# Experts, full batches and cross-attention in one block per engine, and fewer unread products in three pauses

## What is computed

```python
x = x + _L0_xattn_ref(ctx_1024, _layernorm(x))   # distances, dynamic time warping, rows of ctx added along the path
x = x + _L0_ffn_ref(_layernorm(x), gate, W1, b1, W2, b2)   # 16 experts, 3 of them for each row
x = x + _L1_xattn_ref(ctx_1024, _layernorm(x), mask, ...)  # cross-attention over 722 masked rows and the 100 own ones
x = x + _L1_ffn_ref(_layernorm(x), ...)                    # 4 low-rank variants of one layer, the best 2 for each row
```

```python
raw_gate = jax.nn.softmax(jnp.einsum('btd,de->bte', x, gate), axis=-1)
_, topk_idx = jax.lax.top_k(raw_gate, 3)
hidden = jax.nn.relu(jnp.einsum('btd,edh->bteh', x, W1) + b1)
expert_out = jnp.einsum('bteh,ehd->bted', hidden, W2) + b2
return jnp.einsum('bte,bted->btd', gate_topk, expert_out)
```

## Time and profile before

| | |
|---|---|
| median of 3 runs | 1208.29 us (1207.68 to 1208.56) |
| the profiled execution | 1209.34 us, span from first to last instruction 1207.7 us |
| mean granted TensorE clock | 0.950 |
| TensorE (PE) busy | 1074.1 us, 89% of the span |
| VectorE, ScalarE, GpSimd busy | 460.0, 336.7 and 224.6 us |
| DMA traffic | 152.84 MB, mean 127 GB/s |

### The profile page before, as it was taken

One profiled execution on the slowest core, in us unless ns is written; L12 is line 12 of the kernel. 1 busy time (PEld: TensorE's weight loads), 2 busy tenths in 40 slices (PEclk: granted clock), 3 DMA queues, 4 the chain that ended last, 5 costly groups with the idle time before them and its releaser, 6 DMA issues. The chain is left out here.

```text
span 1207.7 us, 17529 instructions
## 1 busy us (share of the span) xinstructions
PE 1074.1 (89%) x5498; PEld 702.9 (58%) x5499; DVE 460.0 (38%) x1698; ACT 336.7 (28%) x802; POOL 224.6 (19%) x341
## 2 busy tenths in 40 slices
PE   8966679937949999999999999949999999999997
PEld 8952235524448777677766777635446665555554
DVE  7847888883570000000000010036765463121212
ACT  4424756770001222222222222214245430000000
POOL 0963021110021121121111111210030001121211
PEclk9978799968969999999999999969999999999999
DMA  8876005128404575856596555560021005000000
GB/s 302 227 169 219 1 1 183 53 99 220 152 14 164 156 246 183 283 193 218 182 311 201 182 182 183 173 196 10 0 77 64 1 1 157 1 1 1 14 14 28
DMA packets 71763, 152.84 MB, mean 127 GB/s; under 512 B 12026, under 2 KB 16258, under 8 KB 70870
## 3 DMA queue, kind: packets, MB, share of 16 engines
q1 hardware_dynamic: 63454, 131.21, 32.0%
q0 software_dynamic: 6928, 17.04, 6.3%
q10 hardware_dynamic: 1320, 3.84, 1.2%
HBM read 131.83 MB, written 20.25 MB: 126 GB/s over the span
## 5 line engine op out<-in xcount | busy, mean ns | idle before, releaser
L1305 ACT ACTIVATE att<-phid,b 128x128 f32<-128x128 f32 x216 | 79.3, 367 | 306.8 <-PE phid L1274 306.8
L1327 DVE TENSOR_TENSOR att<-py,att 128x512 f32<-128x512 f32 x27 | 18.7, 692 | 367.3 <-PE py L1282 367.3
L1274 PEld LDWEIGHTS phid<-tiles,shared 128*128 128x128 f32 x896 | 111.5, 192 | 37.4 <-issue 37.4
L1274 PEld LDWEIGHTS phid<-tiles,Wmem 128*128 128x128 f32 x832 | 103.5, 192 | 39.1 <-issue 39.1
L1274 PE MATMUL phid<-tiles,shared 128*128 x896 | 114.4, 276 | 1.2 <-issue 0.5
L1274 PE MATMUL phid<-tiles,Wmem 128*128 x832 | 106.3, 276 | 5.8 <-issue 4.5
L1282 PE MATMUL py<-shared,att 128*128 128x512 f32 x224 | 110.0, 593 | 0.0
L1282 PE MATMUL py<-Wmem,att 128*128 128x512 f32 x208 | 102.3, 594 | 0.4 <-DMA att<-in_b 0.4
L2365 PE MATMUL acc<-tiles 128*128 128x400 f32 x256 | 90.6, 505 | 0.0
L2431 DVE SCALAR_TENSOR_TENSOR tiles<-bf,shared 128x400 f32<-128x400 f32 x64 | 32.4, 567 | 130.3 <-PE bf L2350 129.6
L2324 PE MATMUL bf<-shared,Wmem 128*128 128x400 f32 x192 | 70.0, 501 | 2.0 <-PEq L49 1.3
(11 more groups left out here) (388 smaller groups left out, 1715.5 us busy)
## 6 DMA issues: line engine op xcount, KB each, us to landing
Wmem<-in_W SPq DMA_DIRECT2D x16, 2048.0 KB, 14.2
shared<-in_W SPq DMA_DIRECT2D x16, 2048.0 KB, 11.9
cT<-in_ctxT SPq DMA_DIRECT2D x8, 1444.0 KB, 11.8
ctx_rows<-in_ctx SPq DMA_DIRECT2D x8, 1280.0 KB
Wmem<-in_Wkv SPq DMA_DIRECT2D x2, 2048.0 KB, 9.2
att<-in_b SPq DMA_DIRECT2D x16, 256.0 KB, 14.3
tiles<-in_WoT SPq DMA_DIRECT2D x4, 1024.0 KB
Wmem<-in_WiT SPq DMA_DIRECT2D x3, 1024.0 KB, 7.1
```

Of the source, the lines that this page charges most:

```text
L1274: ins = pe.matmul(ph[j % NH][:, :], W1[u][:, k, j * P:(j + 1) * P], xgT[:, bass.ds(w, 1), k * P:(k + 1) * P].rearrange("p o t -> p (o t)") ...
L1305: act.activation(hT[:, j, :], ph[j % NH][:, :], ACT.Relu, bias=b1[:, bass.ds((e + u) * HJ + j, 1)]).then_inc(relu_ok, 1)
```

## The change

Four things.

1. `experts` and `attend_full` no longer open blocks. They become `expert_parts` and `full_batches`, which return one function for each engine; `attend` calls them at the head of its own streams. So the two block ends (L1185 and L1880) with their clearings are gone. The banks of PSUM are shared with `attend`'s; the tiles of the full batches lie in the room of the queries.
2. The flag is still read by each engine, now behind its last expert work. If it is not set, the body is branched over. VectorE increments a new semaphore `full_over` behind that, and the four other engines wait for it. TensorE then reads the number of tiles from the table and waits for the last `y_free`. VectorE's two memsets and GpSimd's constant are only made if the flag is set; `qk_scale` is computed on VectorE behind the experts.
3. The unread products ahead of `attend`'s first transpose become 20 (18 before), behind that wait.
4. Three other pauses have fewer: 13 for 18 at the start of `distances`, 12 for 18 ahead of the first path product, 18 for 36 ahead of the table product.

```diff
@@ distances, TensorE
-            keep_awake(pe, pbb[0], ident, 18)
+            keep_awake(pe, pbb[0], ident, 13)
@@ route, TensorE
             pe.wait_ge(p_out[0], 16)
-            keep_awake(pe, px_whole[1], ident, 18)
+            keep_awake(pe, px_whole[1], ident, 12)
...
             pe.wait_ge(over_ok, 1)
-            keep_awake(pe, px_whole[0], ident, 36)
+            keep_awake(pe, px_whole[0], ident, 18)
             pe.wait_ge(of_ok, 2)
@@ experts
-def experts(nc, io, res):
-    ctx = ExitStack()
-    with ctx:
-        sb, pb, sem = allocator(nc, ctx)
+def expert_parts(io, res, sb, sem, bank):
...
-        banks = [pb(f"phid{i}", [P, D]) for i in range(NH)]
-        ph = [bank[:, 0:P] for bank in banks]
-        py = pb("py", [P, D])
-        ptx = [pb(f"ptx{i}", [P, KD * P]) for i in range(2)]
+    ph = [bank[i][:, 0:P] for i in range(NH)]
+    py = bank[4]
+    ptx = bank[5:7]
...
-        block = ctx.enter_context(nc.Block())
...
+    return y_free, expert_sp, expert_pe, expert_act, expert_pool, expert_dve
@@ attend
+        y_free, expert_sp, expert_pe, expert_act, expert_pool, expert_dve = expert_parts(io, res, sb, sem, bank)
+        full_sp, full_pe, full_act, full_pool, full_dve = full_batches(io, res, sb, sem, bank, qT[:, :, :].rearrange("p k n -> p (k n)"))
         block = ctx.enter_context(nc.Block())
...
         def _(sp):
+            expert_sp(sp)
+            full_sp(sp)
...
         def _(pool):
+            expert_pool(pool)
+            full_pool(pool)
...
-            keep_awake(pe, sum_b, ident, 18)
+            expert_pe(pe)
+            full_pe(pe)
+            last = pe.value_load(res["table"][0:1, E_N:E_N + 1], min_val=E_N, max_val=SLOT_TILES)
+            pe.wait_ge(y_free, last + 1)
+            keep_awake(pe, sum_b, ident, 20)
             turn(0)
...
+            expert_act(act)
+            full_act(act)
             root(0)
...
+            expert_dve(dve)
+            dve.wait_ge(res["vec_in"], 48)
+            link(dve.scalar_tensor_tensor(qk_scale[:, :], gammas[:, 0:1], -DH ** -0.5, gammas[:, 1:2], ALU.mult, ALU.mult))
+            full_dve(dve)
             for m in range(B // 2 + 1):
@@ attend_full
-def attend_full(nc, io, res):
+def full_batches(io, res, sb, sem, bank, spare_cols):
...
-        q = sb("q_d", [S, D])
-        qT = sb("qT_d", [P, KD, S])
-        prT = sb("prT_d", [P, NT, S])
-        o, oT = sb("o_d", [S, D]), sb("oT_d", [P, KD, S])
+    q, o = part(D)[0:S, :], part(D)[0:S, :]
+    qT, oT = (part(KD * S).rearrange("p (k s) -> p k s", k=KD) for i in range(2))
+    prT = part(NT * S).rearrange("p (t s) -> p t s", t=NT)
...
-        def each_full(eng, body):
+    def each_full(eng, body, first=None):
             some = eng.value_load(res["flag"][0:1, B:B + 1], min_val=0, max_val=1)
             with eng.If(some == 1):
+            if first is not None:
+                first()
...
             each_full(sp, body)
+        sp.wait_ge(full_over, 1)
...
             each_full(pe, body)
+        pe.wait_ge(full_over, 1)
...
             each_full(act, body)
+        act.wait_ge(full_over, 1)
...
-            each_full(pool, body)
+        each_full(pool, body, first)
+        pool.wait_ge(full_over, 1)
...
-            each_full(dve, body)
+        each_full(dve, body, first)
+        dve.sem_inc(full_over, 1)
@@ build
-        experts(nc, io, res)
-        attend_full(nc, io, res)
         attend(nc, io, res)
```

More of the change, by code:

```diff
@@ new lines, in full_batches, with part @@
+    ident, x_sb = res["ident"], res["x"]
+    Wq, Wkv, Wo = res["Wq"], res["Wkv"], res["Wo"]
+    vec, qk_scale = res["vec"], res["qk_scale"]
+    stats, mv, rstd = sb("stats_d", [P, NT, 6]), sb("mv_d", [P, NT, 2]), sb("rstd_d", [P, NT])
+    spare = [res["tiles"][:, B + i * NT:B + (i + 1) * NT, :] for i in range(3)]
+    rows = spare[0]
+    vals = spare[1]
+    lnT = spare[2].rearrange("p t d -> p (t d)")[:, 0:KD * NKD].rearrange("p (k n) -> p k n", k=KD)
+    cuts = [0]
+    def part(n):
+        cuts.append(cuts[-1] + n)
+        return spare_cols[:, cuts[-2]:cuts[-1]]
@@ new lines, in full_batches @@
+    took = sem("took_d")
+    bt, b0, b1, p0, p1, bo = bank[0:6]
+    d_in, batch_done, pe_turn, dve_turn, ask_act, act_did, ask_pool, pool_did, hset = (sem(n) for n in (
+        "d_in", "batch_done", "pe_turn", "dve_turn", "ask_act", "act_did", "ask_pool", "pool_did", "hset"))
+    full_over = sem("full_over")
+    cols = [P * t for t in range(CT)] + [C]
+    def each_full(eng, body, first=None):
+        some = eng.value_load(res["flag"][0:1, B:B + 1], min_val=0, max_val=1)
+        with eng.If(some == 1):
+            if first is not None:
+                first()
+            with eng.Fori(0, B) as b:
+                f = eng.value_load(res["flag"][0:1, bass.ds(b, 1)], min_val=0, max_val=1)
+                r = eng.value_load(res["runs"][0:1, bass.ds(b, 1)], min_val=0, max_val=B - 1)
+                with eng.If(f == 1):
+                    body(b, r)
@@ new lines, in full_act, with body, full_pool, first @@
+    def full_act(act):
+        def body(b, r):
+            act.wait_ge(ask_act, (HEADS + 1) * r + 1)
+            act.activation(rstd[:, :], rstd[:, :], ACT.Sqrt).then_inc(act_did, 1)
+            for h in range(HEADS):
+                act.wait_ge(ask_act, (HEADS + 1) * r + h + 2)
+                act.activation(pr[:, :], sc[:, :], ACT.Exp, bias=least[:, 0:1], scale=-1.0, accum_out=total[:, h:h + 1]).then_inc(act_did, 1)
+        each_full(act, body)
+        act.wait_ge(full_over, 1)
+    def full_pool(pool):
+        def first():
@@ L2120, in body @@
+            for t in range(NT):
+                take()
+                dve.tensor_copy(rows[0:KR[t], t, :], b0[0:KR[t], :])
+                dve.drain()
+                unit(rows[0:KR[t], t, :], KR[t])
                 give()
                 take()
-                dve.tensor_copy(oT[:, :, :], bt[:, :].rearrange("p (k s) -> p k s", k=KD)[:, :, 0:S])
+                dve.tensor_copy(vals[0:KR[t], t, :], b0[0:KR[t], :])
+                give()
+            take()
+            dve.tensor_copy(q[:, :], b0[0:S, :])
```

645 lines of the change are left out of this document (297 added, 348 removed).

## The result

| | before | after |
|---|---|---|
| median | 1207.99 us (1207.40 to 1208.56, 4 runs) | 1195.30 us (1192.97 to 1196.96, 4 runs) |
| profiled execution, its span | 1209.34, 1207.7 | 1194.54, 1192.9 |
| mean granted TensorE clock | 0.950 | 0.954 |

The ratio of after to before is 0.9894, 95% interval 0.9875 to 0.9912: 12.7 us less by the medians, 10.6 to 15.1 by the interval. The forecast was 14.8 less (1193.5).

What follows compares the result with a forecast made beforehand. TensorE was taken to bound the kernel, with one 18.75 us hole between experts and attention. Terms 9.5 + 4.0 + 1.3 + 0 = 14.8 us gave 1193.5 us against the median shown, 1208.29; range 1190.5 to 1198.5.

Steps and rivals of the forecast that it cites:

- The merge, up to the first turn: Between experts and attention: one block instead of three starts the first turn 9.8 us earlier, 9.5 us kept.
- The landing of x: Start of attention: the first load of x is back 4.5 us after issue, at 793.5, bounded by 792.4 and 798.5.
- The cover: Behind the experts: flag reads and branches (TensorE 4.79 us, VectorE 3.2) lie under GpSimd's scatter, with 0.6 us to spare.
- Rival A: Attention's start: first wait longer through late x, stalls in the open or falling clock; merge gives 4.5 to 7.5; chance 0.20.
- rival E: Attention's start: GpSimd's DRAIN or full_over waits act as a barrier before x; merge gives 2 us or less; chance 0.03.
- The clock term: First value rows: new TensorE pauses may halve the clock for 3 us, 1.5 us lost; 0.3 taken off.
- The table pause: Ahead of the table product: 18 for 36 unread products starts it 4.0 us earlier, GpSimd's third product being late next.
- The path pause: Ahead of the first path product: 12 for 18 unread products ends them 1.27 us earlier, 1.3 us kept.
- The first pause: Start of distances: 13 for 18 unread products gives 0, as ctx's load decides, down to a loss of 0.5 us.
- B: Larger gain: x lands at 792.4 and the clock rises earlier in the routing stage; 1190 to 1191.5 us; chance 0.12.
- C: Three shortened pauses lose the clock; the stage behind pays half of 3 to 7 us; 1195.5 to 1197; chance 0.07.
- D: Expert loops: moved code makes a backward branch fetch, 3.1 us each; slower than before, 1218 us; chance 0.03.

Runs made afterwards that it cites:

- two_blocks: Kernel before without its block of full batches, qk_scale computed behind VectorE's expert work, experts keeping their own block: 1203.06 us, ratio 0.9939 to the kernel before.
- no_flag: Changed kernel without the flag's reads, branches and bodies, a semaphore from VectorE in their place: 1200.88 us, ratio 0.9927 to the kernel before.
- pauses_only: Kernel before with only the three shorter pauses (13, 12 and 18 unread products), no merge: 1205.58 us, ratio 0.9961 to the kernel before.
- filled_b: Changed kernel with 26 unread products for 20 ahead of attention's first turn and 5 behind the first two turns, repeated in the third group: 1198.14 us, ratio 0.9900.
- filled: Changed kernel with 26 unread products for 20 ahead of attention's first turn and 5 more before the first value rows: 1197.87 us, ratio 0.9907 to the kernel before.
- filled_more: Changed kernel with 26 and 5 unread products around attention's first turns, plus 5 ahead of the expert loops and 5 at attention's end: 1197.03 us, ratio 0.9892.
- undo_first: Changed kernel with 18 for 13 unread products at the start of distances: 1197.13 us, ratio 0.9907 to the kernel before.
- control_b: Changed kernel unaltered, measured again in the group of the kernels that put back one old count: 1196.91 us, ratio 0.9907 to the kernel before.
- control: Changed kernel unaltered, measured again beside its two halves: 1200.62 us, ratio 0.9919 to the kernel before.
- merge_only: Changed kernel with the three old counts put back (18, 18, 36) and the merged block kept: 1202.88 us, ratio 0.9935 to the kernel before.
- three undo kernels: Changed kernel with one old count put back each: 18 at the start of distances, 36 ahead of table, 18 ahead of path: 1197.13, 1199.73, 1197.52 us.

## Why the prediction was right, and where it wasn't

**The merge, up to the first turn.** Predicted 9.8, measured 10.28. The load of x as start, TensorE's products 0.1 behind it (0.03), the turn 8.7 behind it (8.16): all there. The landing of x was taken as 4.5 us; it was 3.96 in after and 3.9 to 5.0 over the other merged kernels. The estimate from the earlier trace rows was close though of another transfer, which is some luck. What the step had wrong is its input: it counts from `x_back[0]` alone, and the second pair's load held VectorE in six of eleven profiles. In after it didn't. The page "DMA: Bandwidth & Descriptors" of the Trainium skill (HWDGE ordering), by which each DMA engine consumes the descriptors of x before those of the keys behind them, is not contradicted: with 16 such loads issued from 784 on, the first pair never landed later than 5.0. Whether they delay the second pair (up to 7.31) no run shows.

**The cover.** TensorE's branch was taken as 4.79 and was 3.88; VectorE's `full_over` came 3.8 us behind its last expert work (4.15 taken), of which its branch was 3.0 (3.2). The margin was 1.1 us, 0.6 forecast. two_blocks and no_flag bound it from both sides: the flag's block as a whole, with its memsets, its branches and its end, costs 7.0, and flag and branches behind the experts nothing. Rival A's part of stalls in the open and rival E are out. The page "Runtime: NRT & Kernel Launch" of the Trainium skill (Instruction fetch mechanics), by which a taken branch to code that isn't loaded waits for a fetch, was cited for that stall; the branch stalls on TensorE whether its target is the end of a block (4.79) or the code behind (3.88).

**The clock term: mis-sized.** The step said that 3 us of value rows might run at half speed, 1.5 us lost, but took off only 0.3. Measured: 1.7 to 2.1 when it happens, and it happened in 6 of 8 profiles. The mechanism, its place and its price were named; its likelihood was read from one row (the pause of 1.95 in the earlier trace rows) and set too low. It should have gone into the sum in full: 9.8 - 1.5 = 8.3 for the merge. By the traces the merge is worth 7.0 (behind the load of x), by the medians 6.5 to 7.9: that is about rival A's size (4.5 to 7.5), in after by the last of its three causes and not by the landing or the branches, and beside it by the late fall below.

**What the sum didn't hold.** Short falls of the clock in stages that the change doesn't touch. At the first expert products: from there to the load of x it is 407.2 to 407.9 with the clock kept, 408.4 to 409.2 without it, some 1.2 us, in 8 of the 14 profiles, pauses_only among them (not in before, nor in after). At the pause of 1.00 ahead of the output projection, or that of 1.5 ahead of the feed-forward's first products: 1.2 to 1.9 more than before from the queries to the end (3.2 for two falls), in all eight profiles of merged kernels without fillers, in two_blocks and in filled_b (twice), and not in before, pauses_only, filled and filled_more. The same pause of 1.0 stands in the kernel before without a fall. The count speaks for the merge bringing it about, by the moment at which the pause now comes; filled_b, against filled of the same code, shows that it isn't the code alone. It stays open. With the fall at the value rows (1.7) it is what the first comparison lacks: 12.7 by the medians and 12.80 between the profiles from the path pause on, where 14.8 was forecast. That the profiled spans as a whole differ by 14.8 is luck, a sum of errors: 2.0 more than the change explains ahead of the path pause (the first store of the path lay between 272.4 and 280.7 over the runs, with the same code ahead of it but for one count), 0.7 more at the path, 0.5 more at the turn, against 1.7 and 1.5 of clock.

**The table pause.** Predicted 4.0 with GpSimd late next; 4.17 between the profiles, 3.25 when undone, GpSimd the releaser in every one. What was not seen: the gain depends on when the clock rises under the long version.

**The path pause.** Predicted 1.3; 2.0 between the profiles, 0.64 when undone, for the same reason.

**The first pause.** Predicted 0, "down to a loss of 0.5"; the medians of undo_first and control_b are 0.2 apart, which is nothing. Its risk shows only when ctx comes late: at 16.56 in pauses_only and 17.73 in filled_b the pauses of 1.98 and 2.77 were followed by products 1.6 us longer. With ctx at 15.8 to 16.0 and pauses of 1.2 to 1.6 the clock held, with 13 products (control, control_b) as with 18 (merge_only). No profile with 18 products had ctx as late as 16.56, so what they would have saved isn't shown.

**Rivals.** B (larger): x didn't land before 3.9. C: the mechanism exists (previous paragraph), but none of the three undo kernels was faster than control_b, so it has no price in the medians. The products right behind the path and table pauses ran at full clock. The fall at the first expert products, 1 of 4 with the old table pause and 7 of 9 with the new one, stays a possible price of some 1.2 us. D: the expert stage is as long as before where the clock is alike, 407.47 before and 407.40 after; no fetch in a loop.

**A small miss.** ScalarE's table load was put before the first input. It came behind a wait, as the timeline of ScalarE in the kernel after shows, and the square root behind it was ready at 788.60, just as VectorE went on (788.63): it cost nothing, with no margin.

```profile
787.10 1.28 ACT L1672 ACT_TABLE_LOAD   x1 [15.02 <-DVE rstd_l L1762]
```

## What to carry to other kernels

A block end costs what its slowest engine has still to finish: here 4.48 us of GpSimd's DRAIN behind an indirect DMA and 4.8 us of TensorE's branch over code that isn't used, and in the merged kernel neither is on the path: the DRAIN is gone from this place and the branch lies under a transfer. When a stage is released earlier, look at what TensorE now waits for in small pieces: pauses of 1 to 1.5 us that were hidden behind a late start come into the open, and the clock may take back what it took here, 1.7 of 10.3 us at the first place and 1.2 to 1.9 at a later one. Count that at its full price, not at a fraction. Before a late start is put down to a missing or an added filler, read the releaser of the late row: here it was VectorE behind the loads of x in every merged profile. And products issued to hold the clock should end when the next late input arrives: what goes beyond is path, as the table and path pauses show (3.25 and 0.64 us when undone). The shorter rows cost nothing that the medians here can show; the profiles leave 1.2 us open.

## What was not expected of the hardware

- Pauses of 1.2 to 1.4 us on TensorE were followed by about 3 us at the low clock in most executions and not in others of the same program, with pauses nearly as long (5.34 against 3.65 us for the same eight rows, behind 1.42 and 1.20 us in after and 1.28 and 1.20 in control_b).
- The time until the clock rises behind an idle stretch differs between executions: 72 unread rows took 10.25 to 11.15 us over four profiles, the 24 ahead of the path product 4.90 to 5.49 over ten, the 36 ahead of the table product 5.62 to 6.70 over ten.
- TensorE's branch over a body that is never run takes 3.88 us where the body stands in the attention's block (4.79 before; 3.38 to 3.92 over the other merged kernels); VectorE's 3.0 us. The branches of ScalarE, GpSimd and SyncE over their parts took 0.05 to 0.06 us in the same trace, and GpSimd and SyncE went on within 0.3 us.
- GpSimd's clearing of the semaphores at the end of attention takes 459 ns, where the longest was 333 before; it presumably clears those of three functions at once. The queue row of the kernel after, all six clearings:

```profile
L48 POOLq EVENT_SEMAPHORE_RANGE_CLEAR  x6: 196/243/459, 79.9 to 1192.3; - x6
```
